# A bidirectional Mamba layer on one Trainium2 core: background work at other places of the loop, a third entry in GpSimd's ring, stores issued earlier, loops of four chunks

## The chip, the core and the metric

The kernel runs on one core of one Trainium2 chip. Times are device microseconds of one execution on that core. "Before" is the tuned kernel as it stands; the change is described below.

## The reference, cut to what matters

For two sequences of 4096 rows of 512, a layernorm with modulation, then a Mamba block forward and one over the flipped sequence, projected together, a gated residual, and a second layernorm with a linear layer on weights and activations rounded to a 6-bit grid.

```python
def _mamba(x, win, wconv, bconv, wx, wdt, bdt, Alog, Dp, wout):
    u, z = jnp.split(x @ win.T, 2, axis=-1)                 # 1024 channels each
    u = silu(causal depthwise conv over 4 steps of u + bconv)
    dbc = u @ wx.T                                          # dt (32), B (16), C (16)
    delta = softplus(dt @ wdt.T + bdt)
    dA = exp(delta[..., None] * -exp(Alog))                 # per channel and state
    dBu = (delta * u)[..., None] * Bm[:, :, None, :]
    h = dA_t * h + dBu_t                                    # over 4096 steps, 16 states
    y = einsum(h, C_t) + u * Dp
    return (y * silu(z)) @ wout.T
x = x + ga * (concat([mamba_f(h), flip(mamba_b(flip(h)))]) @ wproj.T + bproj)
x = x + gb * quantized_linear(layernorm(x) * (1 + cb) + sb)
```

## The kernel before, in words

There are three stages. `setup_stage` prepares tables, `final_stage` adds the two directions and does the second half of the layer; the change touches neither. `scan_stage` takes nearly all the time.

**The loop.** The two directions are 32 chunks of T = 512 time steps. A chunk is worked in MT = 8 tiles j of 128 channels, and a tile in NQ = 8 pairs q of the 16 states. One pair is a *position* p = 8 j + q; a chunk has 64. Channels lie on the partitions, time along the free axis. Every engine runs its own program over the same positions and meets the others through semaphores; the loops of all but SyncE (`Fori`, lines 609, 812, 1070 and 1125) hold two chunks a turn, s = 0 and 1. SyncE has a program of its own, also of two chunks a turn.

**One position.** GpSimd multiplies `dBu` for two states (L620). ScalarE makes two `dA` = exp(A delta) (L769) into three PSUM banks in rotation (`dA_bank`). VectorE runs the two scans (L1153), keeps the last column as `state`, and multiplies a state's `h` with the broadcast row `Cb` into `hC` (L1169), a ring of HC = 4. TensorE adds `hC` to the sum `yT` by four transposes (L991). Ten states of sixteen go this way (STRAIGHT). The states 3, 7 and 11 (ASIDE) are scanned by VectorE into the ring `hR` of HR = 2; GpSimd multiplies them in place (L629) and TensorE adds them three pairs later (JOINS). The states 1, 5 and 9 (TURNED) are scanned into `hV`, transposed by TensorE (L968, items T), and multiplied with the column of C by ScalarE into `turned` (L722).

**The background.** All other work of the loop is a table, `SCHEDULE`: items with the positions at which TensorE issues their pieces, and one of three PSUM banks `bg`. An item's name is a kind and a number: U projects a channel tile of the next chunk (L923, four K steps), C is its convolution (L938) on rows that went through DRAM (`pre_scratch`), Z the projection of the gate (L945), D the step size (L973), X and K the B and C rows, O the output projection of the chunk before (L984, eight K steps), H the transposes of new x, Y the turning back of a tile's sum with its skip (L997 to L1006), T the transposes of a TURNED state. At a position TensorE first issues the background pieces and then adds that position's products. A piece waits until the last item in its bank has been taken away.

`TAKE` says at which position ScalarE takes an item out of its bank. "Midway" items are taken between the position's two `dA`, the others behind the second. For D that is `sp_r` and `sp_a` (L651), for C `u` (L679) with an exponential one position on and logarithm and exponential two on, for U `hist` and `pre` (L674, L675), for O `pre`, named `outev` in the code (L731): O and U share the two halves of one buffer.

```python
MIDWAY = ("Z", "T")
TAKE = {name: at[-1] + (2 if name[0] in MIDWAY + ("U",) else 1) for name, at, bank in SCHEDULE}
```

**SyncE's order** is in `chunk` (L412 on), a list by position too. When a U has been taken it stores `pre` (L369), waits for that store (for the first U right there), and loads the four shifted copies for the convolution (L374). A C frees the only place of these copies, so the next C's load follows it. The store of an O (L436) waits until the O has been taken; ScalarE waits for that store before it writes the same half again.

**GpSimd** also finishes `u` (L594), `z` (L598) and the steps `delta` and `du` (L584, L588), the latter at the seventh pair of a tile.

Of the kernel before, what the change touches and what calls it, by code (L numbers as in the profile page):

```python
# [15 lines left out]
N = 16  # L16
# [5 lines left out]
T = 512  # L22
# [27 lines left out]
HC, HR, HV = 4, 2, 2  # L50

AHEAD = 4
# [38 lines left out]
MIDWAY = ("Z", "T")  # L91
TAKE = {name: at[-1] + (2 if name[0] in MIDWAY + ("U",) else 1) for name, at, bank in SCHEDULE}
# [177 lines left out]
def scan_stage(nc, io, dram):  # L270

    with ExitStack() as ctx:
# [80 lines left out]
        dA_bank = lambda s, j, n: (n + s * MT + j) % 3  # L353

        @block.sync
        def _(sp):
# [56 lines left out]
            def chunk(i, s, rows, row0, d, d1, d2):  # L413

                for p in range(POS):
# [22 lines left out]
                    if p == TAKE["O0"] + 1:  # L438

# [124 lines left out]
        def _(pool):  # L564
# [44 lines left out]
            with pool.Fori(0, CHUNKS // 2) as r:  # L609
                for s in range(2):  # L610
                    i = r * 2 + s
                    for j in range(MT):
                        g = i * MT + j
                        pool.wait_ge(du_made, g + 1)
                        for q in range(NQ):
# [21 lines left out]
                            for m in range(MT):  # L637
                                if p == TAKE[f"C{m}"] + 4:
# [6 lines left out]
        def _(act):  # L645
# [112 lines left out]
            def step_dA(g, j, s, n):  # L758
# [3 lines left out]
                else:  # L762
                    before = [k for k in (N - 3, N - 2, N - 1)
                              if dA_bank(*((s, j - 1) if j else (1 - s, MT - 1)), k) == dA_bank(s, j, n)][0]
# [4 lines left out]
                act.activation(dA[dA_bank(s, j, n)][:], delta[:, j % 2, :], ACT.Exp,  # L769
                               scale=A[:, s, j * N + n:j * N + n + 1]).then_inc(dA_made, 1)  # L770
# [41 lines left out]
            with act.Fori(0, CHUNKS // 2) as r:  # L812
                for s in range(2):
                    i = r * 2 + s
                    bank = lambda name: bg[BANK[name]]
                    act.wait_ge(bg_free, freed(i - 1, "K"))
                    act.wait_ge(A_loaded[s], r * 16 + 16)
                    for j in range(MT):
# [3 lines left out]
                        for q in range(NQ):  # L822
                            p = j * NQ + q
                            step_dA(g, j, s, 2 * q)
# [22 lines left out]
                            step_dA(g, j, s, 2 * q + 1)  # L847
# [8 lines left out]
                            for name in BY_ACT:  # L856
# [40 lines left out]
        def _(pe):  # L897
# [172 lines left out]
            with pe.Fori(0, CHUNKS // 2) as r:  # L1070
                for s in range(2):
                    i = r * 2 + s
# [22 lines left out]
        def _(dve):  # L1095
# [29 lines left out]
            with dve.Fori(0, CHUNKS // 2) as r:  # L1125
                for s in range(2):
# [500 lines left out]
```

## Time and profile before

| | us |
|---|---|
| median of 3 runs | 8231.17 |
| lowest and highest | 8225.30, 8234.27 |
| the profiled execution | 8225.38 |
| its span in the profile | 8223.6 |

The profile shows one execution. Busy time of an engine is the time in which one of its instructions runs; "issue" as a releaser means that the engine waited for nothing that the profile shows. `A <- B` in a list of waits reads: A sat idle until B released it. TensorE's clock was granted at 0.949 of its full 2.4 GHz on average. A position takes a little under 4 us, and a line of the timeline may merge equal instructions (x2, x4). A K step of 512 columns shows as two matmuls.

### The profile page before, as it was taken

Reading aid. Unit: us, or ns where it says so; the run is one execution under the profiler, and the core shown is the slowest. Engines: PE = TensorE matmul, PEld = TensorE weight load, DVE = VectorE, ACT = ScalarE, POOL = GpSimd, SP = SyncE. Lnnn points to the kernel's source line nnn. Section 1 sums busy time; section 2 is a strip of 40 time slices with the busy share of each in tenths; the row PEclk is TensorE's granted clock in tenths of the full one; section 3 lists DMA queues with packets and bytes.
Section 4 is the critical chain, followed back from the end, with each engine's and each line's share of the span. In section 5 each row is a group of like instructions: output and inputs, shape, how many; then the busy total and the mean of one; then the engine's idle time right before and its main releaser. Section 6 shows DMA issues by size and latency. Waiting matters only on the chain. (4 is left out here: it accounts for less than half of the span.)

```text
span 8223.6 us, 140600 instructions
## 1 busy us (share of the span) xinstructions
PE 7084.9 (86%) x32680; PEld 4106.4 (50%) x32680; DVE 7419.1 (90%) x11770; ACT 5942.1 (72%) x12302; POOL 7305.9 (89%) x4074
## 2 busy tenths in 40 slices
PE   6888888898888888888888889888888888988788
PEld 3454545555554545555555555555454554545444
DVE  0899999999999989999999999999999999999788
ACT  2777777777777777777777777777777777777644
POOL 1899999999999989999899999999999999989667
PEclk8999999999999999999999999999999999999999
DMA  5443444434443444344344443443344434433544
GB/s 163 133 131 117 125 121 137 139 95 134 123 124 116 124 138 139 93 129 131 116 125 121 139 138 92 133 128 119 115 131 136 132 97 133 127 116 119 169 158 147
DMA packets 597413, 1050.17 MB, mean 128 GB/s; under 512 B 113456, under 2 KB 221872, under 8 KB 588016
## 3 DMA queue, kind: packets, MB, share of 16 engines
q1 hardware_dynamic: 594384, 1038.78, 42.4%
q8 instruction: 313, 5.13, 0.3%
q14 instruction: 636, 5.21, 0.2%
q10 hardware_dynamic: 2080, 1.05, 0.0%
HBM read 909.69 MB, written 129.91 MB: 126 GB/s over the span
## 5 line engine op out<-in xcount | busy, mean ns | idle before, releaser
L620 POOL TENSOR_TENSOR dBu<-Bb,du 128x1024 f32<-128x1024 f32 x2048 | 4796.8, 2360 | 107.6 <-DVE h L1153 65.3
L769 ACT ACTIVATE dA<-delta,A 128x512 f32<-128x512 f32 x4096 | 2833.6, 705 | 563.1 <-DVE hC L1169 303.3
L1153 DVE TENSOR_TENSOR_SCAN h<-dA,state,dBu 128x512 f32<-128x512 f32 x2048 | 2639.9, 1289 | 335.6 <-ACT dA L769 259.7
L991 PE MATMUL yT<-ident,hC 128*128 128x128 f32 x10240 | 1673.7, 293 | 766.5 <-DVE hC L1169 738.4
L991 PEld LDWEIGHTS yT<-ident,hC 128*128 128x128 f32 x10240 | 1217.7, 148 | 1422.6 <-DVE hC L1169 1124.2
L1169 DVE TENSOR_TENSOR hC<-h,Cb 128x512 f32<-128x512 f32 x2048 | 1390.5, 679 | 0.0
L629 POOL TENSOR_TENSOR hR<-hR,Cb 128x512 f32<-128x512 f32 x768 | 976.1, 1271 | 347.3 <-DVE state L1182 337.8
L1153 DVE TENSOR_TENSOR_SCAN hR<-dA,state,dBu 128x512 f32<-128x512 f32 x768 | 974.8, 1269 | 184.3 <-ACT dA L769 112.3
L722 ACT ACTIVATE turned<-bg,CT 128x128 f32<-128x128 f32 x3072 | 879.0, 383 | 230.3 <-PE bg L968 230.3
L984 PE MATMUL bg<-u,comb 128*128 128x512 f32 x2112 | 1016.1, 595 | 14.4 <-ACT pre L731 13.5
L1153 DVE TENSOR_TENSOR_SCAN hV<-dA,state,dBu 128x512 f32<-128x512 f32 x768 | 971.0, 1264 | 43.1 <-PE bg L968 20.7
L923 PE MATMUL bg<-hT,win_u 128*128 128x512 f32 x2112 | 996.2, 606 | 0.9 <-ACT hT L664 0.9
L945 PE MATMUL bg<-hT,win_z 128*128 128x512 f32 x2048 | 958.5, 593 | 0.0
L1153 DVE TENSOR_TENSOR_SCAN dA<-dA,state,dBu 128x512 f32<-128x512 f32 x512 | 648.5, 1267 | 0.0
L923 PEld LDWEIGHTS bg<-hT,win_u 128*128 128x128 f32 x2112 | 386.9, 195 | 408.9 <-issue 407.6
L991 PEld LDWEIGHTS yT<-ident,hR 128*128 128x128 f32 x3072 | 376.7, 148 | 416.6 <-issue 364.2
L968 PEld LDWEIGHTS bg<-ident,hV 128*128 128x128 f32 x3072 | 371.1, 142 | 296.4 <-issue 242.9
L945 PEld LDWEIGHTS bg<-hT,win_z 128*128 128x128 f32 x2048 | 359.9, 191 | 305.4 <-issue 305.4
L991 PE MATMUL yT<-ident,hR 128*128 128x128 f32 x3072 | 512.3, 292 | 0.0
L968 PE MATMUL bg<-ident,hV 128*128 128x128 f32 x3072 | 474.0, 278 | 29.1 <-DVE u L1113 23.9
L984 PEld LDWEIGHTS bg<-u,comb 128*128 128x128 f32 x2112 | 356.8, 191 | 250.8 <-issue 229.7
L1002 PEld LDWEIGHTS bg<-ident,turned 128*128 128x128 f32 x3084 | 379.7, 148 | 161.2 <-issue 161.2
(163 smaller groups left out, 9366.3 us busy)
## 6 DMA issues: line engine op xcount, KB each, us to landing
comb<-pre_scratch SPq DMA_DIRECT2D x1040, 256.0 KB, 4.6
Bb<-bc_scratch SPq DMA_DIRECT2D x264, 512.0 KB, 8.2
Cb<-bc_scratch SPq DMA_DIRECT2D x264, 512.0 KB, 7.3
win_u<-in_win SPq DMA_DIRECT2D x264, 256.0 KB, 3.6
pre_scratch<-pre SPq DMA_DIRECT2D x264, 256.0 KB, 5.1
comb<-comb_scratch SPq DMA_DIRECT2D x66, 1024.0 KB, 7.2
win_z<-in_win SPq DMA_DIRECT2D x257, 256.0 KB, 2.7
part_scratch<-pre SPq DMA_DIRECT2D x132, 256.0 KB, 2.0
```

What stands on the lines that cost most here:

```text
L620: pool.tensor_tensor(dBu[:, q % AHEAD], Bb[:, 2 * q:2 * q + 2, :], du[:, j % 2, :].unsqueeze(1).broadcast_to([P, 2, T]), ALU.mult).then_in ...
L629: pool.tensor_tensor(hR[:, k, :], hR[:, k, :], Cb[:, n, :], ALU.mult).then_inc(hR_made, 1)
L722: ins = act.mul(turned[:, TURNED.index(n), tt * P:(tt + 1) * P], bank[:, tt * P:(tt + 1) * P], CT[:, s, tt, n:n + 1])
L769: act.activation(dA[dA_bank(s, j, n)][:], delta[:, j % 2, :], ACT.Exp, scale=A[:, s, j * N + n:j * N + n + 1]).then_inc(dA_made, 1)
L923: ins = nc.tensor.matmul(bank[:], win_u[:, m % RING, k, :], hT[:, slot, k, :], start=(k == 0), stop=(k == KD - 1))
L945: ins = nc.tensor.matmul(bank[:], win_z[:, j % 2, k, :], hT[:, slot, k, :], start=(k == 0), stop=(k == KD - 1))
L968: ins = nc.tensor.matmul(bank[:, tt * P:(tt + 1) * P], hV[:, (j * NT + TURNED.index(n)) % HV, tt * P:(tt + 1) * P], ident[:], start=True, ...
L984: ins = nc.tensor.matmul(bank[:], comb[:, m, tt * P:(tt + 1) * P], u[:, s, m, :], start=(k == 0), stop=(k == MT - 1))
L991: ins = nc.tensor.matmul(yT[:, tt * P:(tt + 1) * P], product[:, tt * P:(tt + 1) * P], ident[:], start=first and tt == 0, stop=False, is_tr ...
L1002: nc.tensor.matmul(bank[:, tt * P:(tt + 1) * P], turned[:, k, tt * P:(tt + 1) * P], ident[:], start=False, stop=False, is_transpose=True, ...
L1153: nc.vector.tensor_tensor_scan(to, dA[dA_bank(s, j, n)][:], dBu[:, q % AHEAD, k, :], state[:, c:c + 1], ALU.mult, ALU.add).then_inc(h_made, 1)
L1169: nc.vector.tensor_tensor(hC[:, (j * NS + STRAIGHT.index(n)) % HC, :], bank[:], Cb[:, n, :], ALU.mult).then_inc(hC_made, 1)
```

## The change

Six parts: (a) HR, the ring of `hR`, from 2 to 3 entries. (b) SyncE stores an O at the position at which it is taken, no longer one later, and `cur` is loaded a position earlier. (c) C and D are taken two positions after their last piece instead of one, T behind the second `dA` instead of midway; GpSimd's `finish_u` moves to five positions after the take (four for the last). (d) `GENERAL` gives every item new positions and some another bank. (e) As a result of (c) and (d) the distance from a U's take to its C changes. (f) The loops of GpSimd, ScalarE, TensorE and VectorE hold four chunks a turn. SyncE's loops stay.

The old positions 32 to 36 hold, in this order: Y3, U4; T, C2; Z4; T, half of U5; half of U5, C3. The new 17 to 21: O3 (two steps), half of Z2, T; the same without T; O3 (two steps), T; U0; T, U1. The new 40 to 43: Y4, half of Z5; half of Z5, T, U6; nothing; T, C5, U7. C6 stays at 45 with U6 taken at 43, and U0 is taken at 22.

```diff
-HC, HR, HV = 4, 2, 2
+HC, HR, HV = 4, 3, 2
+
+TURN = 4
 
 AHEAD = 4
...
-    ("D1", (0,), 0), ("Z0", (1, 2), 1), ("O0", (2, 3, 3, 4, 4, 5, 6, 6), 0), ("D2", (7,), 1),
...
-    ("D3", (15,), 1), ("Z2", (17, 18), 1), ("O3", (18, 18, 19, 19, 20, 20, 21, 22), 0), ("U0", (20, 21), 1),
-    ("D4", (23,), 1), ("U1", (23, 24), 0), ("Z3", (25, 26), 1), ("C0", (26,), 0), ("U2", (28, 28), 0),
...
+    ("O3", (15, 15, 17, 17, 18, 18, 19, 19), 0), ("Z2", (17, 18), 1), ("U0", (20, 20), 1), ("U1", (21, 21), 0),
+    ("D4", (23,), 1), ("C0", (24,), 0), ("Z3", (25, 26), 1), ("U2", (26, 26), 0), ("C1", (28,), 0),
...
-MIDWAY = ("Z", "T")
-TAKE = {name: at[-1] + (2 if name[0] in MIDWAY + ("U",) else 1) for name, at, bank in SCHEDULE}
+MIDWAY = ("Z",)
+TAKE = {name: at[-1] + (2 if name[0] in "ZTUCD" else 1) for name, at, bank in SCHEDULE}
...
-                        if p == TAKE[f"O{tt}"] + 1:
+                        if p == TAKE[f"O{tt}"]:
                             sp.wait_ge(bg_free, freed(i, f"O{tt}"))
...
-            with pool.Fori(0, CHUNKS // 2) as r:
-                for s in range(2):
-                    i = r * 2 + s
+            with pool.Fori(0, CHUNKS // TURN) as r:
+                for v in range(TURN):
+                    i, s = r * TURN + v, v % 2
...
-                                if p == TAKE[f"C{m}"] + 4:
+                                if p == TAKE[f"C{m}"] + (5 if m < MT - 1 else 4):
                                     finish_u(i + 1, 1 - s, m)
...
-                                if p == TAKE[name] and name[0] == "T":
-                                    take_turned(ready(i, name), bank(name), int(name[1:]) % N, s)
...
+                                if kind == "T":
+                                    take_turned(ready(i, name), bank(name), k % N, s)
```

**TensorE, positions 24 and 25 of a chunk, where C0 comes.** Rows are issued instructions in order; L938 is the convolution, L945 a K step pair of Z3, L968 a T, L991 an addition to `yT`. Before, C0 stands at position 26, after all of Z3:

```order
L945 MATMUL bg<-hT,win_z 128x512 x2
L966 ISA
L968 MATMUL bg<-ident,hV 128x128 x4
L1085 REGISTER_ALU
L991 MATMUL yT<-ident,hC 128x128 x4
L945 MATMUL bg<-hT,win_z 128x512 x2
L904 REGISTER_ALU
L936 ISA
L938 MATMUL bg<-comb,wtap 32x512 x4
L1085 REGISTER_ALU
L991 MATMUL yT<-ident,hC 128x128 x4
```

After the change (all lines are two higher) it stands at position 24, right behind Y2, whose last transposes are the first row (the second half of Z3 follows the last):

```order
L1008 MATMUL bg<-ident,yt 128x128 x4
L906 REGISTER_ALU
L938 ISA
L940 MATMUL bg<-comb,wtap 32x512 x4
L1087 ISA
L993 MATMUL yT<-ident,hC 128x128 x4
L906 REGISTER_ALU
L947 MATMUL bg<-hT,win_z 128x512 x2
L968 ISA
L970 MATMUL bg<-ident,hV 128x128 x4
L1087 REGISTER_ALU
L993 MATMUL yT<-ident,hC 128x128 x4
```

Moved: C0 is issued two positions earlier, ahead of Z3 and of the T of position 25.

**ScalarE, positions 39 and 40, where C4's result is taken.** L769 is a `dA`, L722 the taking of a T, L679 that of a C, L693 a later step of C3. Before:

```order
L769 ACTIVATE dA<-delta,A 128x512
L720 REGISTER_ALU
L722 ACTIVATE turned<-bg,CT 128x128 x4
L693 ACTIVATE su<-su 128x512
L761 REGISTER_ALU
L769 ACTIVATE dA<-delta,A 128x512
L678 REGISTER_ALU
L679 ACTIVATE u<-bg,bconv 128x512
L766 REGISTER_ALU
```

After:

```order
L771 ACTIVATE dA<-delta,A 128x512
L722 REGISTER_ALU
L724 ACTIVATE turned<-bg,CT 128x128 x4
L768 REGISTER_ALU
L771 ACTIVATE dA<-delta,A 128x512
L770 ISA
L771 ACTIVATE dA<-delta,A 128x512
L680 REGISTER_ALU
L681 ACTIVATE u<-bg,bconv 128x512
L768 REGISTER_ALU
```

Moved: the taking of the T stands behind the second `dA` of position 39, and C4's `u` one position and two `dA` later.

**SyncE, where O3 is stored.** L436 stores an O, L369 a U's `pre`, L459 loads A, L374 loads the rows of a convolution. Before, from U0's store on:

```order
L454 REGISTER_ALU
L369 DMA pre_scratch<-pre 128x512
L458 ISA
L459 DMA A<-A_scratch 128x128
L460 ISA
L374 DMA comb<-pre_scratch 32x4x512 x4
L435 REGISTER_ALU
L436 ISA
L436 DMA part_scratch<-pre 128x512
```

After, from O3's store on (all lines two higher):

```order
L438 ISA
L438 DMA part_scratch<-pre 128x512
L453 REGISTER_ALU
L364 DMA win_u<-in_win 128x512
L428 ISA
L428 DMA gain<-gain_scratch 128x8
L456 REGISTER_ALU
L371 DMA pre_scratch<-pre 128x512
L460 ISA
L461 DMA A<-A_scratch 128x128
L462 ISA
L376 DMA comb<-pre_scratch 32x4x512 x4
```

Moved: the store of O3 was behind U0's store, the wait for it (L460) and the four loads; now it is ahead of all of them.

## Rows read from the trace of the kernel before

**Rows 1.** The page: span, and busy us of each engine (share of the span)
```profile
span 8223.6 us, 140600 instructions
...
PE 7084.9 (86%) x32680; PEld 4106.4 (50%) x32680; DVE 7419.1 (90%) x11770; ACT 5942.1 (72%) x12302; POOL 7305.9 (89%) x4074
```

**Rows 2.** Two chunks: length; busy PE, PEld, DVE, ACT, POOL; clock, DMA share, GB/s
```profile
2574.48:2806.34 231.86, 205.40 (x960) 120.17 (x960) 219.33 (x353) 176.63 (x367) 220.00 (x124) 0.95 0.41 118
2806.34:3045.71 239.37, 205.00 (x969) 118.97 (x968) 219.47 (x354) 179.13 (x371) 216.89 (x120) 0.95 0.43 130
```

**Rows 3.** VectorE's waits: us in total, times, longest
```profile
DVE h L1153 <- ACT dA L769: 259.7, 150, 99.1
DVE hR L1153 <- ACT dA L769: 112.3, 187, 1.7
DVE h L1153 <- issue: 73.7, 15, 5.0
DVE hR L1153 <- PE yT L991: 71.7, 75, 1.8
...
DVE u L1113 <- PE bg L1006: 35.2, 62, 3.4
```

**Rows 4.** Timeline, first scan of three chunks on VectorE: start, length; [idle before]
```profile
2574.48 1.29 DVE L1153 TENSOR_TENSOR_SCAN h<-dA,state,dBu 128x512 f32<-128x512 f32 x1 [4.90 <-issue]
...
2806.34 1.28 DVE L1153 TENSOR_TENSOR_SCAN h<-dA,state,dBu 128x512 f32<-128x512 f32 x1
...
3045.71 1.29 DVE L1153 TENSOR_TENSOR_SCAN h<-dA,state,dBu 128x512 f32<-128x512 f32 x1 [4.97 <-issue]
```

**Rows 5.** ScalarE's waits
```profile
ACT sp_r L651 <- PE bg L973: 304.1, 135, 6.5
...
ACT u L679 <- PE bg L938: 302.9, 147, 5.6
ACT turned L722 <- PE bg L968: 230.3, 128, 4.8
...
ACT hist L674 <- DMA part_scratch<-pre: 162.3, 32, 6.7
```

**Rows 6.** Timeline at the store of O3: SyncE's queue, ScalarE, VectorE
```profile
2886.84 0.37 SPq L369 DMA_DIRECT2D pre_scratch<-pre  x1
...
2893.40 1.76 SPq L374 DMA_DIRECT2D comb<-pre_scratch  x4
2895.42 0.36 SPq L436 DMA_DIRECT2D part_scratch<-pre  x1
...
2901.13 0.26 ACT L674 ACTIVATE hist<-bg,cur 128x3 f32<-128x3 f32 x1 [6.72 <-DMA part_scratch<-pre]
...
2902.58 1.29 DVE L1153 TENSOR_TENSOR_SCAN h<-dA,state,dBu 128x512 f32<-128x512 f32 x1 [3.01 <-ACT dA L769]
```

**Rows 7.** Timeline at C4: TensorE, ScalarE, VectorE
```profile
2711.84 3.60 PE L923 MATMUL bg<-hT,win_u 128*128 128x512 f32 x8
2716.11 1.06 PE L938 MATMUL bg<-comb,wtap 128*32 128x512 f32 x8 [0.67 <-DMA comb<-pre_scratch]
...
2717.24 0.69 ACT L679 ACTIVATE u<-bg,bconv 128x512 f32<-128x512 f32 x1 [1.60 <-PE bg L938]
...
2722.69 1.29 DVE L1153 TENSOR_TENSOR_SCAN h<-dA,state,dBu 128x512 f32<-128x512 f32 x1 [0.84 <-ACT dA L769]
```

**Rows 8.** TensorE's timeline: start, length, what
```profile
2871.10 1.88 PE L984 MATMUL bg<-u,comb 128*128 128x512 f32 x4
2872.81 0.60 PE L991 MATMUL yT<-ident,hC 128*128 128x128 f32 x4
2873.25 1.88 PE L984 MATMUL bg<-u,comb 128*128 128x512 f32 x4
...
2907.11 5.09 PE L923 MATMUL bg<-hT,win_u 128*128 128x512 f32 x8
```

**Rows 9.** The page's DMA issues: median us to landing
```profile
comb<-pre_scratch SPq DMA_DIRECT2D x1040, 256.0 KB, 4.6
```

More of the change, by code:

```diff
@@ L352, in scan_stage @@
         IN_PLACE = [n for n in STRAIGHT if n % 2]
-        dA_bank = lambda s, j, n: (n + s * MT + j) % 3
+        dA_bank = lambda v, j, n: (n + v * MT + j) % 3
         @block.sync
@@ L437, in chunk @@
                                          outev[:, tt % 2, :]).then_inc(out_stored[tt % 2], 16)
-                    if p == TAKE["O0"] + 1:
+                    if p == TAKE["O0"]:
                         sp.dma_start(cur[:], dram["modt"][:, 2:, :][:, bass.ds(i, 1), :].rearrange("p a c -> p (a c)")).then_inc(cur_loaded, 16)
@@ L756, in normalize, with step_dA @@
                                bias=nb[:, tt:tt + 1]).then_inc(ln_done, 1)
-            def step_dA(g, j, s, n):
+            def step_dA(g, j, v, n):
                 if n >= 3:
@@ L763, in step_dA @@
                     before = [k for k in (N - 3, N - 2, N - 1)
-                              if dA_bank(*((s, j - 1) if j else (1 - s, MT - 1)), k) == dA_bank(s, j, n)][0]
+                              if dA_bank(*((v, j - 1) if j else ((v - 1) % TURN, MT - 1)), k) == dA_bank(v, j, n)][0]
                     if before in IN_PLACE:
@@ L768, in step_dA @@
                         act.wait_ge(h_made, g * N - N + before + 1 + H0)
-                act.activation(dA[dA_bank(s, j, n)][:], delta[:, j % 2, :], ACT.Exp,
-                               scale=A[:, s, j * N + n:j * N + n + 1]).then_inc(dA_made, 1)
+                act.activation(dA[dA_bank(v, j, n)][:], delta[:, j % 2, :], ACT.Exp,
+                               scale=A[:, v % 2, j * N + n:j * N + n + 1]).then_inc(dA_made, 1)
             nc.scalar.preload_act_table_set(EXP_LN)
@@ L811, in _ @@
             act.wait_ge(bg_free, PRO)
-            with act.Fori(0, CHUNKS // 2) as r:
-                for s in range(2):
-                    i = r * 2 + s
+            with act.Fori(0, CHUNKS // TURN) as r:
+                for v in range(TURN):
+                    i, s = r * TURN + v, v % 2
                     bank = lambda name: bg[BANK[name]]
                     act.wait_ge(bg_free, freed(i - 1, "K"))
-                    act.wait_ge(A_loaded[s], r * 16 + 16)
+                    act.wait_ge(A_loaded[s], r * (8 * TURN) + (v // 2 * 16 + 16))
                     for j in range(MT):
@@ L823, in _ @@
                             p = j * NQ + q
-                            step_dA(g, j, s, 2 * q)
+                            step_dA(g, j, v, 2 * q)
                             if q == 1:
@@ L846, in _ @@
                                 rstd_exp(i + 2)
-                            step_dA(g, j, s, 2 * q + 1)
+                            step_dA(g, j, v, 2 * q + 1)
                             if q == 5:
@@ L1069, in _ @@
             pe.wait_ge(bg_free, PRO)
-            with pe.Fori(0, CHUNKS // 2) as r:
-                for s in range(2):
-                    i = r * 2 + s
+            with pe.Fori(0, CHUNKS // TURN) as r:
+                for v in range(TURN):
+                    i, s = r * TURN + v, v % 2
                     for j in range(MT):
@@ L1124, in _ @@
                 row_stats(c)
-            with dve.Fori(0, CHUNKS // 2) as r:
-                for s in range(2):
-                    i = r * 2 + s
+            with dve.Fori(0, CHUNKS // TURN) as r:
+                for v in range(TURN):
+                    i, s = r * TURN + v, v % 2
                     for j in range(MT):
@@ L1148, in _ @@
                                 elif n in IN_PLACE:
-                                    to = dA[dA_bank(s, j, n)][:]
+                                    to = dA[dA_bank(v, j, n)][:]
                                 else:
@@ L1152, in _ @@
                                     to = h[:]
-                                nc.vector.tensor_tensor_scan(to, dA[dA_bank(s, j, n)][:], dBu[:, q % AHEAD, k, :],
+                                nc.vector.tensor_tensor_scan(to, dA[dA_bank(v, j, n)][:], dBu[:, q % AHEAD, k, :],
                                                              state[:, c:c + 1], ALU.mult, ALU.add).then_inc(h_made, 1)
@@ L1167, in _ @@
                                     dve.wait_ge(C_loaded[q], i * 16 + 16)
-                                bank = dA[dA_bank(s, j, n)] if n in IN_PLACE else h
+                                bank = dA[dA_bank(v, j, n)] if n in IN_PLACE else h
                                 nc.vector.tensor_tensor(hC[:, (j * NS + STRAIGHT.index(n)) % HC, :], bank[:],
```

2 lines of the change are left out of this document (1 added, 1 removed), and 13 rows, old and new, of the table GENERAL.

## Prediction

> **What bounds the kernel now.** I read the page's busy shares first, then two consecutive chunks cut out of the trace, then the waits of each engine, and last the timeline at single places. VectorE is busy for 7419 of 8224 us and GpSimd for 7306 [rows 1]. In one chunk of 231.9 us VectorE works 219.3, GpSimd 220.0, TensorE 205.4 and ScalarE 176.6; in the next, which takes 239.4, the work is the same [rows 2]. So 219.4 us is the floor that VectorE sets for a chunk as long as its instructions stay as they are, GpSimd (218.5 on average) lies just under it, and TensorE has some 14 us of room. The change alters no instruction of VectorE, so what it can win is VectorE's idle time in the loop. The reader should see in rows 3 where that is: it waits for ScalarE's `dA` 259.7 and 112.3 us (99.1 of the first is one wait ahead of the loop), for TensorE's use of `hR` 71.7, for the gate's bank 35.2, and 73.7 for "issue" in 15 waits. Without the last these are 160.6 + 112.3 + 71.7 + 35.2 = 380 us, **11.9 us a chunk** over 32 chunks; smaller waits I leave aside, as staying.
>
> Why is `dA` late? ScalarE is busy for three quarters of a chunk only, but its queue is in order: it waits for TensorE's results `sp_r` (D) 2.3 us a time, `u` (C) 2.1, `turned` (T) 1.8, and 162.3 us in 32 waits for a store [rows 5], and the `dA` behind stand still. It has three banks of `dA`, so only a stall of more than about a position (219.4 / 64 = 3.4 us) less what it must still do reaches VectorE. Of these 1000 us (and some smaller waits) 273 reached it.
>
> **The changes, one by one.** (a) **Third place in the `hR` ring.** VectorE's scan into `hR` waits until TensorE has added the product two entries back. With three entries and three such states in a tile, it is the entry of a tile before, 8 positions ago; TensorE is never so late. The 71.7 us go [rows 3]. GpSimd multiplies in place as before, same count.
>
> (b) **Stores ahead of the loads.** In the old order SyncE stores O3 one position after it was taken, behind the store of U0, the wait for that store and four loads: U0's store is issued at 2886.84, the loads from 2893.40, O3's store only at 2895.42; ScalarE, which needs O3's buffer for U1, stands for 6.72 us until 2901.13, and VectorE for 3.01 [rows 6]. Now O3 is taken three positions before U1, and its store is the first thing SyncE does at that position. The 162.3 us on ScalarE end; what VectorE loses there (about 1 to 3 us a chunk) is part of the 273 above. Next late is TensorE's U1 itself.
>
> (c) **Later takes.** D and C are taken two positions after their last piece instead of one, T after the second `dA` of the same position instead of before it. At C4 TensorE runs U6 until its load lands (0.67 us of wait), issues the convolution at 2716.11, ScalarE waits 1.60 us for it, VectorE then 0.84 [rows 7]. A position more is 3.4 us, above the means of 2.1 and 2.3. For T the shift is one `dA`, some 0.7 us (an operation of the same size takes 0.69 [rows 7]), and whatever that `dA` waits. The exps and logarithms behind move along; the last is due at GpSimd's `steps` at the tile's seventh pair, still three positions away, and `finish_u` is moved by two. I cost these at nothing: GpSimd runs two to four positions ahead of VectorE, and if that cover went, a late `steps` would hold `dA` for all of the next tile.
>
> (d) **New places on TensorE.** From rows 8 a pair of K steps costs 1.72 us and a product, or the transposes of a T, 0.44 (start to start); a convolution is 1.06 [rows 7], a U 3.44, and a turn back, one K step and sixteen transposes of a quarter product, about 0.86 + 16 x 0.11 = 2.6. The old positions 32 to 36 carry 6.5 + 1.9 + 3.9 + 2.6 + 3.6 = 18.5 us against 5 x 3.4 = 17.2, in a stretch that was already behind. The new ones are light there, but 17 to 21 carry 4.3 + 3.9 + 2.6 + 4.3 + 4.3 = 19.4 in 17.2, and 40 to 43 carry 4.8 + 6.0 + 0.4 + 5.3 = 16.5 in 13.7. The total is the same; TensorE falls 2 to 3 us behind at each peak, and U1 and U6 are taken two positions later, which just about covers that.
>
> (e) **Loads that get less time.** From U0's store to landed rows is 6.6 us to the issue of the loads, 1.8 to issue four, and a median of 4.6 to landing [rows 6, 9], about 12.5. C0 now comes two positions after U0 was taken (three before), C6 two after U6. TensorE does 2.6 us of other work first at C0; I put a wait of 2 to 4 us on TensorE at each of the two. `hC` has four places, three positions of VectorE, so most of it is hidden.
>
> (f) **Four chunks a turn.** At a turn VectorE shows 4.90 or 4.97 us of "issue" [rows 4]; the chunk that starts inside a turn's body has none. 15 turns become 7, and 8 x 4.9 = **39 us** go. The instructions run are the same, so what is fetched in all should be too. The row decides for me, since the gap is there at every second chunk and at no other; what an engine does in it no row says. The Trainium skill (Advanced Engine Details and Errata, Control Flow Timing) gives a compare-and-branch about 0.11 us; by that alone eight branches are worth 1 us and not 39, which speaks against this part of the change.
>
> **The sum.** VectorE keeps idle time at the new peaks: 1.2 us a chunk at positions 20 to 23, 0.8 around C0, 0.4 at 33 to 36, 0.8 around U6 and C6, 0.8 at the tail (C7, X, K) where the places hardly changed. These are my choices, each between nothing (covered by the three banks) and the 1 to 3 us that one such place costs now [rows 6, 7]. That is 4 us a chunk, 128 of the 380. Gain: 380 - 128 + 39 = 291 us. The profiled execution took 8225 with a span of 8224, 6 us under the median of the runs, 8231; setup and final stage are untouched. 8231 - 291 = **7940**. With 7 us a chunk left over it is 8231 - 156 - 39 = 8036, with 1 us 8231 - 348 - 39 = 7844.
>
> **Rivals.** *TensorE becomes the bound.* For it: 205 us of work in a chunk that shall take 225, two peaks, two short loads, and one U that took 5.09 us where another took 3.60, right after TensorE had waited [rows 7, 8]: waiting makes it slower. Against: 14 us of room. Then 9 us a chunk stay: 8231 - 92 - 39 = 8100. *Nearly all idle time goes*, since each peak is within the cover: 7844. *The turn's gap is not the jump* but the engines' alignment, which comes back elsewhere: 8231 - 252 = 7979. That is about the time by the figure of the Trainium skill's page named above. *Nothing moves*, because GpSimd at 218 us a chunk, slowed by its own waits, takes over: within 0.2% (16 us, about what a measurement of this kernel can tell from no change).
>
> *Slower:* the bank of T. The three T of a tile share bank 2, and TensorE may write T5 only once ScalarE has taken T1, now after the second `dA` of the very position at which TensorE wants the bank, T9 likewise. That is 16 places a chunk. The price of one is at least the `dA` of 0.7 us and at most that and the 1.8 us that ScalarE waits for a T today [rows 5]; in the middle 1.6, so 26 us a chunk on an engine with 14 to spare. It decides if ScalarE is less than about 1 us ahead of TensorE at these places. From 9.1 us a chunk passed on, it eats the gain; at half of 26 it is 8231 - 291 + 416 = 8356. Against: TensorE follows VectorE and ScalarE precedes it, so there are some 3 us between, and no wait of TensorE for `turned` is among the rows that matter.
>
> **Chances.** Forecast (7860 to 8040) 0.63; all idle time gone 0.11; TensorE the bound 0.15; turns worth nothing 0.05; no change 0.02; slower 0.04. The first four make 0.94 faster, 0.02 same, 0.04 slower. The range takes half of the "all gone" case and most of the TensorE case: 7860 to 8090.
>
> **What would show it.** After: no wait of `hR` for PE's `yT` over 5 us; no "hist <- DMA part_scratch"; 7 waits of about 4.9 us for "issue"; VectorE's busy time in a chunk still 219 us and the chunk at 224 to 226; the waits for `dA` together under 150 us, sitting near positions 20 to 23 and 41 to 47; TensorE waiting for the `pre_scratch` loads at C0 and C6. I am wrong if the `dA` waits stay over 250 us, if VectorE's own instructions get longer, or if GpSimd's `dBu` shows up as what VectorE waits for.

## The result: 7832 us, 396 us less than before

The kernel before takes 8228.24 us (median of 4 runs, 8224.76 to 8234.27), the changed one 7832.29 (4 runs, 7825.59 to 7834.85). The ratio is 0.9517, with the 95% interval [0.9502, 0.9532]. The forecast was 7940 with a range of 7860 to 8090: the direction was right and the gain of 291 us too small by 105. The nearest of the cases was "nearly all idle time goes", 7844, and the result lies even under that.

The page of the changed kernel, span and busy time, to be held against [rows 1], and the DMA issue that answers to [rows 9]:

```profile
span 7832.9 us, 140448 instructions
...
PE 6926.4 (88%) x32680; PEld 4049.9 (52%) x32680; DVE 7360.3 (94%) x11770; ACT 5962.0 (76%) x12302; POOL 7301.4 (93%) x4074
...
comb<-pre_scratch SPq DMA_DIRECT2D x1040, 256.0 KB, 4.5
```

VectorE has the same 11770 instructions, but its busy time fell from 7419.1 to 7360.3 us. That is something that the prediction had excluded. The loads land as fast as before.

Where the 396 us are, by stretches: from the first to the last scan of the loop, in the view of windows (start and end; length; busy time of PE, PEld, DVE, ACT, POOL; granted clock, DMA share, GB/s). First the kernel before:

```profile
232.12:7748.59 7516.47, 6555.42 (x30840) 3820.43 (x30838) 7019.23 (x11291) 5691.12 (x11807) 6983.15 (x3870) 0.95 0.42 125
```

Then the changed kernel: the loop, one chunk without a turn, one with a turn:

```profile
235.47:7356.46 7120.99, 6392.80 (x30840) 3763.61 (x30838) 6959.85 (x11291) 5710.96 (x11807) 6978.31 (x3870) 0.97 0.45 131
1348.20:1569.27 221.07, 199.25 (x964) 117.78 (x964) 217.47 (x355) 178.71 (x369) 217.84 (x121) 0.97 0.45 132
1789.68:2016.27 226.59, 203.54 (x969) 120.92 (x968) 217.87 (x354) 179.35 (x371) 217.24 (x121) 0.94 0.46 137
```

The loop is 395.5 us shorter, so setup and final stage gave nothing (the two spans differ by 390.7; the one wait ahead of the loop is 5.4 longer). In the loop VectorE's idle time fell from 497.2 us (7516.47 - 7019.23) to 161.1, and its busy time by 59.4. A chunk without a turn takes 221.1 us instead of 231.9 [rows 2], the one that ends at a turn 5.5 more; the mean of the 32 is 222.5, where it was 234.9.

VectorE's waits, against [rows 3]:

```profile
DVE h L1155 <- ACT dA L771: 194.2, 37, 104.5
...
DVE h L1155 <- issue: 34.1, 7, 5.0
...
DVE u L1115 <- PE bg L1008: 13.1, 13, 3.4
...
DVE hV L1155 <- ACT dA L771: 11.8, 19, 0.8
...
DVE hR L1155 <- ACT dA L771: 2.8, 6, 0.6
```

The wait of `hR` for TensorE's `yT` is gone, the one of `hR` for `dA` went from 187 times to 6, the one for the gate's bank from 62 to 13. Of the 194.2 us, 104.5 are the one wait ahead of the loop. Left are 89.7 us in 36 waits, and 84.9 of them, in 29 waits, lie at one position, 55.

The turn, on VectorE's timeline, answers to [rows 4]:

```profile
1124.33 1.29 DVE L1155 TENSOR_TENSOR_SCAN h<-dA,state,dBu 128x512 f32<-128x512 f32 x1 [4.92 <-issue]
```

ScalarE's waits, against [rows 5]. The waits for `turned` are down to 4.9 us in all and no line with `part_scratch` is left:

```profile
ACT hist L676 <- PE bg L925: 95.4, 114, 6.0
...
ACT u L681 <- PE bg L940: 41.0, 19, 6.3
...
ACT sp_r L653 <- PE bg L975: 27.1, 16, 3.2
```

TensorE's waits. The second row was 65.6 us in 36 before, and the third was not among the rows that mattered:

```profile
PE yT L993 <- DVE hC L1171: 358.2, 319, 2.1
PE bg L940 <- DMA comb<-pre_scratch: 173.6, 99, 6.2
PE bg L956 <- POOL u L596: 119.8, 33, 4.8
```

So TensorE's room shrank from 738.4 us of waiting for `hC` (643 times) to 358.2, and it now waits 108 us more for the loads: at C6 85.7 us in 32 waits where there was none, at C0 16.7 us in 26; at C4 it is 52.0, but it was 47.2 before. Hardly any of that reached VectorE: at positions 44 to 47 it waits 3.0 us in all, and apart from the turns and position 55 no group of its waits in the loop comes to more than 14 us.

**The new largest wait.** Timeline of the changed kernel at position 55, of TensorE, GpSimd, ScalarE and VectorE, in order of time:

```profile
2197.13 1.93 PE L956 MATMUL bg<-u,wx 128*64 128x512 f32 x4
...
2200.41 1.26 POOL L586 TENSOR_TENSOR delta<-sp_a,sp_r 128x512 f32<-128x512 f32 x1
...
2201.75 1.26 POOL L590 TENSOR_TENSOR du<-delta,u 128x512 f32<-128x512 f32 x1
...
2202.97 1.26 POOL L596 TENSOR_TENSOR u<-u,su 128x512 f32<-128x512 f32 x1
...
2204.29 3.30 PE L956 MATMUL bg<-u,wx 128*64 128x512 f32 x4 [4.20 <-POOL u L596]
...
2207.62 0.58 ACT L713 COPY dbc<-bg 64x512 f32<-64x512 f32 x1 [4.95 <-PE bg L956]
...
2209.01 1.29 DVE L1155 TENSOR_TENSOR_SCAN h<-dA,state,dBu 128x512 f32<-128x512 f32 x1 [3.35 <-ACT dA L771]
```

GpSimd's `finish_u` of the last convolution (L596) is now six positions behind C7, at 54 and no longer at 53, because C is taken one later and `finish_u` is counted from the take. There it stands behind the two products of `steps`. X's last piece needs that `u`, and the new table has moved it the other way, from 54 to 53. TensorE waits 4.20 us, then takes 3.30 us for four matmuls where those of the piece before took 1.93; ScalarE stands for 4.95 before `dbc`, and VectorE for 3.35. It takes both moves: in the run with the old table below, where X's last piece is at 54, TensorE waits for this `u` once only, 4.2 us, ahead of the loop. The prediction had put the shift of `finish_u` at nothing and looked only at who comes behind the exps, not at X.

### The profile page after: what moved, and what is told of

It is laid out like the page before. It is cut to its first block and busy times, and to the rows that moved or that the text cites. A ratio compares the mean times of both kernels' runs of the same rounds, so it can differ in the third digit from the quotient of the medians.

```text
span 7832.9 us, 140448 instructions
## 1 busy us (share of the span) xinstructions
PE 6926.4 (88%) x32680; PEld 4049.9 (52%) x32680; DVE 7360.3 (94%) x11770; ACT 5962.0 (76%) x12302; POOL 7301.4 (93%) x4074
## 5 line engine op out<-in xcount | busy, mean ns | idle before, releaser
L1155 DVE TENSOR_TENSOR_SCAN h<-dA,state,dBu 128x512 f32<-128x512 f32 x2048 | 2641.3, 1290 | 230.2 <-ACT dA L771 194.2
L993 PE MATMUL yT<-ident,hC 128*128 128x128 f32 x10240 | 1590.5, 284 | 378.4 <-DVE hC L1171 358.2
L993 PEld LDWEIGHTS yT<-ident,hC 128*128 128x128 f32 x10240 | 1196.2, 144 | 901.0 <-DVE hC L1171 570.5
L986 PE MATMUL bg<-u,comb 128*128 128x512 f32 x2112 | 996.0, 595 | 2.5 <-ACT pre L733 1.1
L925 PE MATMUL bg<-hT,win_u 128*128 128x512 f32 x2112 | 968.7, 599 | 0.9 <-ACT hT L666 0.9
L940 PE MATMUL bg<-comb,wtap 128*32 128x512 f32 x2080 | 304.0, 659 | 173.7 <-DMA comb<-pre_scratch 173.6
```

The lines of the kernel that those rows point to most:

```text
L925: ins = nc.tensor.matmul(bank[:], win_u[:, m % RING, k, :], hT[:, slot, k, :], start=(k == 0), stop=(k == KD - 1))
L940: ins = nc.tensor.matmul(bank[j * GROUP:(j + 1) * GROUP, :], wtap[:, m % RING, j, :], place[:, j, :], start=True, stop=True)
L986: ins = nc.tensor.matmul(bank[:], comb[:, m, tt * P:(tt + 1) * P], u[:, s, m, :], start=(k == 0), stop=(k == MT - 1))
L993: ins = nc.tensor.matmul(yT[:, tt * P:(tt + 1) * P], product[:, tt * P:(tt + 1) * P], ident[:], start=first and tt == 0, stop=False, is_tr ...
L1155: nc.vector.tensor_tensor_scan(to, dA[dA_bank(v, j, n)][:], dBu[:, q % AHEAD, k, :], state[:, c:c + 1], ALU.mult, ALU.add).then_inc(h_made, 1)
```

## The experiments

All times are medians of runs beside the kernel before on the same chip; that one's medians are 8220 to 8235 us. "After" is the changed kernel, 7832. An interval of a ratio is some 14 us to either side, so differences between two runs of under 20 us say little. Where two runs come from different chips, "by the ratios" gives their difference worked out from the ratios.

### Undoing one part at a time

**Two chunks a turn.**

```diff
-TURN = 4
+TURN = 2
```

> The changed kernel with loops of two chunks a turn again, nothing else. Theory A (a turn costs VectorE its 4.9 us wait for "issue", and what the waits of a turn hide is not given back): 15 such waits instead of 7, 8 x 4.9 = 39 us more, about 7871 against 7832. VectorE's busy time in the loop stays at 6960 us. Rival (a branch costs about 0.1 us and the gap is the engines' alignment): within 10 us of 7832.

Measured: 7891.96, ratio 0.9589 [0.9573, 0.9605], so 60 us more. VectorE's waits:

```profile
DVE h L1155 <- ACT dA L771: 207.2, 37, 102.2
DVE h L1155 <- issue: 73.5, 15, 5.0
...
DVE u L1115 <- PE bg L1008: 28.9, 20, 4.9
```

The wait is as the first theory has it: 15 times 4.9 us are back, 39.4 us more. But the time is 60. Part of the rest shows in other waits: the gate's bank costs 16 us more, `dA` 15 more (without the first wait). A turn stops TensorE too, for 5.8 us (86.9 us in 15 against 39.7 in 7); that it is the restart with overdue work which costs the rest is argued from these rows, not tested. The rival, under 10 us, is out.

**Two places in GpSimd's ring.**

```diff
-HC, HR, HV = 4, 3, 2
+HC, HR, HV = 4, 2, 2
```

> The changed kernel with two entries in the hR ring. Theory A (the ring is a term of its own, 71.7 us before): VectorE waits again for TensorE's yT at hR, 50 to 75 us in all, and the time is 50 to 90 us over 7832. Rival (it was TensorE's backlog at the old places that made the ring short, and the new places cure it alone): under 15 us.

Measured: 7906.67, 0.9610 [0.9594, 0.9626], 74 us more.

```profile
DVE hR L1155 <- PE yT L993: 103.6, 84, 1.5
```

The time is as the first theory has it. The wait is longer than it was before the change (71.7), and than the 50 to 75 us expected; that this is because less else delays VectorE is argued.

**Takes of C and D one position earlier, `finish_u` with them.**

```diff
-TAKE = {name: at[-1] + (2 if name[0] in "ZTUCD" else 1) for name, at, bank in SCHEDULE}
+TAKE = {name: at[-1] + (2 if name[0] in "ZTU" else 1) for name, at, bank in SCHEDULE}
...
-                                if p == TAKE[f"C{m}"] + (5 if m < MT - 1 else 4):
+                                if p == TAKE[f"C{m}"] + 4:
```

> The changed kernel with C and D taken one position after their last piece instead of two (finish_u four positions after the take), T as in the change. Theory A (the later take is what frees ScalarE's queue): ScalarE waits 1 to 2 us at most C and D again, VectorE for dA 60 to 150 us more, and its busy time grows by about 0.1 us for each new wait: 80 to 170 us over 7832. Rival (the new places on TensorE removed the stalls): under 30 us.

Measured: 7843.45, 0.9534 [0.9516, 0.9551]: 11 us more. The stalls of ScalarE come back nearly as they were [rows 5]:

```profile
ACT u L681 <- PE bg L940: 248.3, 148, 5.7
ACT sp_r L653 <- PE bg L975: 205.9, 129, 5.8
```

VectorE feels them:

```profile
DVE h L1155 <- ACT dA L771: 159.7, 100, 101.1
```

Without the wait ahead of the loop these are 58.6 us, with those of `hV` and `hR` (22.2 and 17.4) 98.2. The changed kernel has 104.3 of them, 84.9 of these at position 55, where none are left now, since `finish_u` is back at 53. Elsewhere the waits for `dA` have grown from 19.4 us to 98.2, by 79, as the first theory said (60 to 150). So this edit takes away two things, a gain and a loss, and its 11 us fall into the rival's range without the rival's reason. What the later takes of C and D are worth at the new places shows beside the run with only the last `finish_u` at 53 (below, 7781.67): 62 us, 68 by the ratios.

**The old table of places, all else new.** `GENERAL` is that of the kernel before.

> The changed kernel with the old table of places, everything else as changed. Theory A (later takes, ring and stores bring most, the places a smaller part): 60 to 120 us over 7832, the waits for dA near the old peak of positions 32 to 43. Rival (TensorE's places are the main term): 150 to 250 us over 7832.

Measured: 7933.85, 0.9638 [0.9622, 0.9655], 102 us more, within the first theory's range. Of 114 us of waits for `dA` in the loop 80 lie at positions 33 to 42, near the old peak, and 34 at 52. VectorE's waits, and one of TensorE's:

```profile
DVE u L1115 <- PE bg L1008: 60.2, 50, 5.0
DVE hV L1155 <- ACT dA L771: 59.9, 98, 2.0
DVE hR L1155 <- ACT dA L771: 45.7, 35, 2.8
...
DVE hV L1155 <- PE bg L970: 38.0, 32, 2.5
```

```profile
PE bg L970 <- ACT turned L724: 60.3, 72, 1.6
```

The last row is the slower rival in person: TensorE does wait for ScalarE to take the T before, in 72 places. With the new table that wait does not show.

**The old table and all the old takes**, so that of the change only the ring, the stores and the turns are left.

> The changed kernel with the old table of places and the old takes (C and D one position after the last piece, T between the two dA): only the third hR entry, the earlier stores and the four-chunk turns are left of the change. Theory B (formed after the first four runs: the later takes are worth 11 us with the new places, but stand in for them where the places are old; places and takes cover each other): 7970 to 8060, so 40 to 120 us over the 7934 of old places with new takes. Rival (the takes are worth 11 us anywhere): 7935 to 7955.

Measured: 8109.25, 0.9850 [0.9833, 0.9866], 120 us under before. At the old places the later takes are worth 8109 - 7934 = 175 us. At the new places two kernels with a ring of three and two chunks a turn can be compared, 7938.53 with the old takes (below) and 7891.96 with the new (above; they differ in the stores too, which are worth nothing there, as the next run shows): 47 us, 53 by the ratios. In the second VectorE idles 100.9 us at position 55, in the first not at all; with the 51 us that the early `finish_u` gives back (below) the takes are worth about 100 there, an estimate. The late take is a cover for a TensorE that is behind; the new table leaves less to cover, but not little. The nearest of the ranges given ended at 8060: I had let the parts cover each other too little.

**The stores of O one position later.**

```diff
-                        if p == TAKE[f"O{tt}"]:
+                        if p == TAKE[f"O{tt}"] + 1:
...
-                    if p == TAKE["O0"]:
+                    if p == TAKE["O0"] + 1:
```

> The changed kernel with the stores of O one position after the take again, as before. Now O3 is taken at 20, so even the later store goes out at 21, ahead of U0's at 22. Theory A (what matters is that the store is ahead of U0's store and loads): within 15 us of 7832, no wait hist <- DMA part_scratch over 10 us. Rival (the store's own position matters): ScalarE waits for part_scratch at O or U again, 40 us or more over 7832.

Measured: 7826.18, 0.9510 [0.9494, 0.9526], no difference, as the first theory said. Here too the store of O3 goes out ahead of U0's store and loads, since O3 is taken at 20; the run shows only that one position more does not matter. What ended the wait for `part_scratch` [rows 5] shows in other runs. With the old table and the stores at the take (the two runs above) no such wait is left; with the new table alone (below), stores one position behind the take, none either. Of the old table with the old stores 149.5 us in 30 waits are left (four chunks a turn alone, below). So either is enough: the store ahead of the loads, or O3's earlier place, which puts it ahead of them.

**T taken between the two `dA` again.**

```diff
-MIDWAY = ("Z",)
+MIDWAY = ("Z", "T")
```

> The changed kernel with T taken between the two dA again. Theory: T's own term is small with the new places; TensorE is ready 1 us after ScalarE asks in many places, so ScalarE waits for turned again (100 to 250 us in all), of which VectorE sees 10 to 40: 7842 to 7872. Rival (the prediction's slower case: the later take makes TensorE wait for bank 2): faster than 7832 by 10 us or more, with no PE <- ACT turned left.

Measured: 7863.01, 0.9564 [0.9548, 0.9580], 31 us more, as expected. Most of ScalarE's wait comes back (187 of 230 us), and VectorE loses a little in 79 places:

```profile
ACT turned L724 <- PE bg L970: 187.4, 215, 1.6
```

```profile
DVE hR L1155 <- ACT dA L771: 33.6, 79, 0.9
```

At position 55 it idles 50.7 us instead of 84.9, so that its idle time in the loop is 161 us as in the changed kernel. The loop of the profiled execution is 17 us longer, all of it busy time of VectorE, which has 170 waits in the loop instead of 95; why a wait adds to busy time is told below.

The single undoings cost 60 + 74 + 11 + 102 + 0 + 31 = 278 us, where the whole change gave 396: the parts are not a sum, and the 11 among them is a gain of 62 with a loss of 51 taken off.

### Doing one part alone, on the kernel before

**The new table alone**, old takes, ring, stores and turns.

> The kernel before with the new table of places alone (hR ring of two, stores a position after the take, old takes, two chunks a turn). Theory B: the table alone brings the stores ahead of U0's and spreads TensorE's work, but the ring (74 us) and the turns (60 us) are missing and the old takes cost little with it: 7832 + 74 + 60 + 11 + T's take 0 to 30, so 7975 to 8010. Rival (the parts only pay together): over 8080.

Measured: 7967.61, 0.9677 [0.9660, 0.9694], 261 us less, a little more than the nearest range given (from 7975). Alone the table brings two thirds of the whole gain; as the last part to be added it brings 102. VectorE waits for `hR` of TensorE 89.0 us now, more than before:

```profile
DVE h L1153 <- ACT dA L769: 150.1, 48, 99.3
DVE hR L1153 <- PE yT L991: 89.0, 70, 1.5
```

**The third ring place alone.** This tests the 71.7 us that the prediction booked as a term of its own.

> The kernel before with three entries in the hR ring, nothing else. The prediction's own term: the 71.7 us that VectorE waits for yT at hR go, 8159. Theory C (each wait that goes also gives back about 0.13 us of overlap between VectorE's instructions that the profile books as busy time: 75 waits, 10 us): 8150. Rival (VectorE gets to the next late dA sooner and waits there): 8175 to 8210, with the waits for dA up by 20 to 50 us.

Measured: 8229.01 over 10 runs beside a median of 8220.26, ratio 1.0001 [0.9988, 1.0013]. Nothing, with up to 10 us either way, and no theory had that (they gave 8150 to 8210), though the wait is gone:

```profile
DVE h L1153 <- ACT dA L769: 296.3, 167, 103.0
DVE hR L1153 <- ACT dA L769: 122.5, 213, 1.7
...
DVE u L1113 <- PE bg L1006: 69.7, 64, 3.4
```

Against [rows 3] the waits for `dA` grew by 33 (without the one ahead of the loop) and 10 us and the one for the gate's bank by 35, together 77 for 71.7 gained. A VectorE that does not wait for TensorE at `hR` arrives earlier at the next thing that TensorE or ScalarE has late.

**The ring in two more settings**: old table with new takes and two ring places, and new table with old takes and three.

> The changed kernel with the old table of places and two entries in the hR ring; new takes, stores and turns stay. Old places with the ring of three took 7934. Theory E (the third entry is worth nothing only while the dA behind it is late; the new takes make dA punctual, so it pays also at the old places): 50 to 100 us more, 7985 to 8035, VectorE waiting 60 us or more for yT at hR. Rival (the third entry pays only with the new places): under 15 us more, 7920 to 7950.

> The kernel before with the new table and three entries in the hR ring; old takes, two-chunk turns. The new table alone took 7968 with 89 us of waits for yT at hR. Theory E: the new places too make dA punctual, so the entry pays: 50 to 90 us less, 7880 to 7920. Rival (only the new takes let it pay): under 15 us, 7955 to 7985.

Measured: 7949.60, 0.9672 [0.9655, 0.9689], against 7933.85 with three places; and 7938.53, 0.9654 [0.9637, 0.9671], against 7967.61 with two. The third place's worth is

| | old takes | new takes |
|---|---|---|
| old table | 0 (old stores and turns) | 16 |
| new table | 29 (old stores and turns) | 74 |

By the ratios the 16 is 28 and the 29 is 19, so these two can't be told apart; only 0 and 74 are clear of the rest. Theory E's 50 to 100 us came in neither time. At the old places the result lies in the rival's range, at the new ones between the two. VectorE's waits show the hand-over. At the old places with the new takes, the third entry ends 73.9 us of waits for `yT`, and the gate's bank grows from 24.0 us to 60.2, `hR` for `dA` from 24.1 to 45.7, `hV` for `dA` from 52.8 to 59.9. At the new places with the old takes it ends the 89.0 us, and `hR` for `dA` grows from 26.6 to 87.0. A fixed price is out; the place is worth its wait only where little else is late.

**Four chunks a turn alone.**

```diff
-            with pool.Fori(0, CHUNKS // 2) as r:
-                for s in range(2):
-                    i = r * 2 + s
+            with pool.Fori(0, CHUNKS // TURN) as r:
+                for v in range(TURN):
+                    i, s = r * TURN + v, v % 2
```

and the same on ScalarE, TensorE and VectorE, with `TURN = 4`.

> The kernel before with four chunks a turn, nothing else. The prediction's own term: 8 waits for issue of 4.9 us go, 39 us, 8192. Theory D (from the run with two-chunk turns in the changed kernel, 60 us for 8 turns): each turn costs 7.5 us, since the engines also restart one after the other; 8170. Rival (in the old kernel the restart is hidden by ScalarE's waits that come anyway): 8190 to 8215.

Measured: 8166.84 beside 8220.26, 0.9926 [0.9909, 0.9944]: 53 us less for eight turns, 6.7 each (7.5 in the new setting, which is the same within the intervals). This is the one part whose worth hardly depends on the others.

### Beyond both kernels

**`finish_u` of the last tile one position earlier**, against the wait at position 55.

```diff
-                                if p == TAKE[f"C{m}"] + (5 if m < MT - 1 else 4):
+                                if p == TAKE[f"C{m}"] + (5 if m < MT - 1 else 3):
```

> The changed kernel with GpSimd's finish_u of the last tile one position earlier, three after the take instead of four, ahead of the steps of that position. VectorE's largest remaining wait, 84.9 us at position 55, comes from X, whose last piece on TensorE waits for this u (119.8 us in 33 waits). Theory: TensorE's wait for u falls under 30 us and the time by 40 to 80 us, to 7750 to 7790. Rival (GpSimd then waits for ScalarE's sigmoid of C7 instead, and with it dBu): no gain, or up to 20 us slower, with POOL u <- ACT su over 100 us.

Measured: 7781.67, 0.9451 [0.9436, 0.9467], 51 us less than after, as the theory has it. TensorE's wait at X is one left at the start, and the waits of VectorE for ScalarE's `dA` are almost nothing (the first of the loop, 101.5, is now listed under GpSimd):

```profile
PE bg L956 <- POOL u L596: 4.2, 1, 4.2
```

```profile
DVE h L1155 <- POOL dBu L622: 102.9, 2, 101.5
DVE h L1155 <- issue: 52.1, 20, 5.3
...
DVE h L1155 <- ACT dA L771: 9.0, 15, 1.7
```

Of the 20 waits for "issue" seven are the turns; the other 13, 16.8 us, stand at position 55. So 23.9 of the 84.9 us are left there, listed for the greater part under another name.

**The same with eight, and with sixteen chunks a turn.**

> The changed kernel with the early last finish_u and eight chunks a turn: 3 turns instead of 7. Theory D: 4 x 7.5 = 30 us under the 7782 of the early finish_u alone, 7752, with three waits for issue. Rival (a longer body costs at each turn in proportion): 7775 to 7785.

> The changed kernel with the early last finish_u and sixteen chunks a turn: one turn boundary instead of three. With theory D (7.5 us a turn) 15 us under the 7757 of eight chunks a turn, 7742. Rival (the price grows with the length of the body, or the first fetch of a longer body does): 7755 or more.

Measured: 7756.62, 0.9430 [0.9415, 0.9446], and **7734.90, 0.9409 [0.9394, 0.9425]**, the best of all: 490 us under before. Four turns fewer gave 25 us, two more fewer gave 22 (17 and 17 by the ratios). Differences of that size say little about the price of one turn, but a price that grows with the length of the body (the rivals' 7775 and 7755 or more) is out. TensorE's wait at the turn, with eight chunks and with sixteen:

```profile
PE bg L999 <- issue: 17.4, 3, 6.5
```

```profile
PE bg L999 <- issue: 6.0, 1, 6.0
```

With sixteen VectorE has 18.3 us of "issue" left, in 11 waits, of which one is the turn (5.5), and is busy for 7360.4 of 7741.8 us: 95%.

## Why the prediction was right and wrong

**Right in kind.** The time went where the argument said: out of VectorE's idle time in the loop. Its signs came in: no wait of `hR` for `yT`, none of `hist` for `part_scratch`, seven waits of 4.9 us for "issue", the `dA` waits under 150 us but for the first, longer waits of TensorE for the loads. Three did not: the chunk is at 222.5 on average, not 224 to 226; VectorE's busy time in it is not 219; and the waits for `dA` do not sit near positions 20 to 23 and 41 to 47, but at 55. The new places on TensorE (part d) are the largest single part: 261 us alone, 102 when all else is there. "TensorE becomes the bound" is out: it still waits 358 us for `hC`.

**The step that failed: "219.4 us is the floor that VectorE sets for a chunk as long as its instructions stay as they are".** In a chunk the same instructions now show 217.5 us. An instruction that follows the last at once starts before the other's end is recorded; one that follows a wait does not. Kernel before, VectorE's timeline:

```profile
2885.58 1.28 DVE L1153 TENSOR_TENSOR_SCAN h<-dA,state,dBu 128x512 f32<-128x512 f32 x1
2886.77 1.27 DVE L1153 TENSOR_TENSOR_SCAN dA<-dA,state,dBu 128x512 f32<-128x512 f32 x1
2887.94 0.67 DVE L1169 TENSOR_TENSOR hC<-h,Cb 128x512 f32<-128x512 f32 x1
```

The second starts 0.09 us before 2885.58 + 1.28, the third 0.10 before the second's end. So a wait costs some 0.1 us more than its idle time, booked as busy time. In this pair the instructions did not get shorter: the recorded lengths of VectorE's instructions in the loop add up to 7831 us before and 7832 after, while the overlap of neighbours in the records grew from 811 to 871. In other runs these lengths add up to as little as 7807, so how the price of a wait divides into lost overlap and longer records is open; the busy time itself is what was counted. The kernel before has 552 listed waits in the loop, the changed one 95; 58.8 us of busy time over 457 waits are 0.13 each. The runs between lie near that line: 7410.9 us busy at 464 waits (old table and takes), 7375.3 at 242 (old table), 7367.8 at 169 (two ring places); of all seventeen kernels none is more than 8 us off it. Many short waits are dearer than they look, and this was the largest piece that the sum lacked.

**The other terms**, against the 395.5 us of the loop:

| term | forecast | measured |
|---|---|---|
| booked waits in all | 380 | 380 |
| of these left over | 128 | 106 (`dA` 89.7, bank 13.1, `hR` 2.8) |
| turns, as "issue" | 39 | 39.6 |
| smaller waits | "leave aside, as staying" | 44 before, 21 after: 22 |
| VectorE's busy time | "alters no instruction" | 59 |
| gain | 291 | 395 |

The last column is 274 + 40 + 22 + 59. So 59 us of the 105 are the failed step, 22 the small waits (which hang on the same TensorE and ScalarE as the booked ones and had no reason to stay), 22 the estimate of what is left.

**The estimate of the leftovers was right in size by luck.** I put 4 us a chunk on five places: positions 20 to 23, C0, 33 to 36, C6 and the tail (C7, X, K). Measured are 3.3, but most of it at one place, position 55. That is in the tail, which I had at 0.8 "where the places hardly changed" and which lost 2.7 there, for a reason that (c) had costed at nothing ("`finish_u` is moved by two"; for the last tile it is one, against an X that comes one earlier). At the other four, 3.2 us together in the forecast, VectorE lost about half a microsecond a chunk: 12.9 us in all at 33 and 36, 3.0 at 44, nothing at 20 to 24. The work at 17 to 21, which I had as 19.4 us in 17.2, cost VectorE nothing there; that the later takes and the banks cover it is argued.

**(a) The ring** was booked as 71.7 us that "go". Alone it is worth nothing, with everything else 74. The number fits this change only because the rest of the change was there: it may be subtracted only in a sum that clears the other waits too.

**(b) The stores.** The wait ended, as forecast. The order of the stores ends it at the old places, O3's new place ends it with the old order; in this change either would have done.

**(c) The takes** cover much, as forecast, 175 us at the old places and at the new ones 62 for C and D and 31 for T. That they cost nothing is wrong in one place, the last `finish_u`: 51 us.

**(e) The short loads.** I expected 2 to 4 us of waiting at C0 and at C6, 32 times each, 128 to 256 us. TensorE's waits for the loads grew by 108: 2.7 us a time at C6, as expected, but only 16.7 us in all at C0. (The three terms from the store to the landed rows add up to 13.0, where the text says about 12.5.) VectorE did not feel them; that they fell into TensorE's room (the 738 us of waiting for `hC`) is argued.

**(f) The turns.** The row decided rightly against the figure of the Trainium skill (Advanced Engine Details and Errata, Control Flow Timing, about 0.11 us for a compare-and-branch): the rival "alignment" is out, since the waits and the time came and went with the number of jumps in four runs. The term was under-sized: over eight turns one costs 6.7 to 7.5 us, its 4.9 and some 2 to 3 more, which the other waits of the run with two chunks a turn hold. The same page of the Trainium skill (ISA Cache) says that the instruction cache has two lines of 256 instructions. By that rule the target of a jump back over VectorE's 700 instructions of two chunks would not be there. That fits a wait of 4.9 us whether the body is two chunks long or four; no run here tests the mechanism.

**The slower rival.** The bank of T is a real wait: 60.3 us in 72 places with the old table and the new takes. Its price of 1.6 us a place was its longest, 0.8 the mean, and it struck 72 places, not 512. With the new table it is not among TensorE's waits that matter.

## What to carry to other kernels

Count a bounding engine's waits, not only their microseconds: each of some 457 waits that went gave 0.13 us beyond its idle time here. The idle time behind one releaser is no price of a repair: with in-order engines that are all a little late, removing one wait hands its time to the next (the ring: 0, 16, 29, 74 us, of which only the first and the last stand clear of the noise), and what one part is worth depends on the others. An undoing that takes back a loss along with a gain shows only their difference (the takes of C and D: 11 us, and 62 once the loss is held apart). Where a take is moved later, follow everything counted from it to its first reader; here one such shift, met by a reader moved forward, cost 51 us that a single number gave back.

## What the runs showed of the hardware

- Loops: at each turn VectorE shows 4.9 to 5.1 us of "issue" (5.5 at the one turn of the sixteen-chunk body) and TensorE 5.5 to 6.0, with bodies of two, four, eight and sixteen chunks. Going from 15 turns to 7, 3 and 1 gave 60, 25 and 22 us (59, 17 and 17 by the ratios).
- Back-to-back instructions of VectorE overlap in the records by 0.06 to 0.10 us, 0.08 on average; after a wait they don't.
- TensorE after a wait of 4.20 us: the granted clock was 0.58 in the stretch behind it, mostly the level of 1.2 GHz, against 1.00 (2.4 GHz) for the same four matmuls a few microseconds earlier; they took 3.30 us instead of 1.93. Columns as above:

```profile
2197.10:2199.10 2.00, 2.00 (x6) 0.57 (x6) 2.00 (x5) 2.00 (x5) 2.00 (x1) 1.00 0.00 0
2204.29:2207.60 3.31, 3.31 (x5) 0.83 (x6) 1.37 (x5) 0.00 (x0) 3.31 (x2) 0.58 0.00 0
```

So of the 4.95 us that ScalarE stood before `dbc`, about 1.4 (3.30 - 1.93) were the clock, and here the wait of TensorE cost its user more than the wait.
